# Inverted residual: the remaining 32 channels' taps on TensorE for four blocks at once, and VectorE on the second 128 channels' taps in every block but the last

## The reference

```
def _L3_conv_ref(x, w1, ..., w2, ...):          # x: (8, 48, 64, 64)
    h = relu(bn(einsum('oc,bchw->bohw', w1, x)))           # expand 48 -> 288 channels
    h = conv3x3(h, wd, padding=1, feature_group_count=288) # depthwise, one 3x3 filter a channel
    h = relu(bn(h))
    h = bn(einsum('oc,bchw->bohw', w2, h))                 # reduce 288 -> 48
    return x + h
```

## Time and profile before

| what | value |
|---|---|
| median of three runs | 1986.39 us |
| the profiled execution's own time / its span | 1985.13 / 1983.2 us |
| from the first to the last block's end in this stage | 1547.99 to 1979.00 us of the span |
| TensorE / VectorE / ScalarE busy in those 431.01 us | 399.37 / 282.46 / 170.33 us |
| mean granted TensorE clock there | 0.97 |

### The profile page before, as it was taken

One profiled execution on the slowest core, in us unless ns is written; L12 is line 12 of the kernel. 1 busy time (PEld: TensorE's weight loads), 2 busy tenths in 40 slices (PEclk: granted clock), 3 DMA queues, 4 the chain that ended last, 5 costly groups with the idle time before them and its releaser, 6 DMA issues. The chain is left out here.

```text
span 1983.2 us, 41167 instructions
## 1 busy us (share of the span) xinstructions
PE 1589.4 (80%) x13002; PEld 935.5 (47%) x13002; DVE 1475.4 (74%) x2699; ACT 1172.0 (59%) x2257; POOL 642.3 (32%) x577
## 2 busy tenths in 40 slices
PE   8979248888888888704888888888860899999997
PEld 6535125555555555203555555555520344445444
DVE  4539978888888888646888888888856766666666
ACT  1116128888888888543888888888853344444431
POOL 2010035555555555203555555555500000000000
PEclk9989669999999999857999999999985799999999
DMA  3769366666666666666666666667576011011100
GB/s 108 254 196 211 97 137 108 108 106 107 107 107 107 107 106 91 113 147 131 106 107 107 107 107 107 107 108 108 81 121 164 14 34 34 21 31 35 35 19 25
DMA packets 132266, 199.40 MB, mean 101 GB/s; under 512 B 28528, under 2 KB 47824, under 8 KB 131920
## 3 DMA queue, kind: packets, MB, share of 16 engines
q1 hardware_dynamic: 132176, 198.08, 53.7%
HBM read 73.72 MB, written 37.75 MB: 56 GB/s over the span
## 5 line engine op out<-in xcount | busy, mean ns | idle before, releaser
L720 PE MATMUL gates_l<-xh_l,w_l 128*112 128x512 f32 x3072 | 801.5, 409 | 122.3 <-ACT xh_l L757 122.1
L720 PEld LDWEIGHTS gates_l<-xh_l,w_l 128*112 128x112 f32 x3072 | 500.3, 175 | 422.8 <-issue 288.8
L684 POOL TENSOR_TENSOR xh_l<-hs,xh_l 48x512 fp32r<-48x512 f32 x252 | 300.5, 1192 | 442.0 <-ACT xh_l L757 442.0
L693 POOL TENSOR_TENSOR xh_l<-xf_l,xs_l 48x512 fp32r<-48x512 f32 x256 | 311.7, 1217 | 33.2 <-DVE xs_l L809 32.8
L720 PE MATMUL gates_l<-xc_l,w_l 128*112 128x512 f32 x512 | 164.6, 403 | 135.1 <-DVE begun_l L829 135.1
L853 DVE TENSOR_TENSOR hs<-gate_o_l,tanh_c_l 48x256 f32 (+1 forms) x512 | 193.3, 416 | 73.9 <-ACT tanh_c_l L786 70.1
L1292 PE MATMUL b_dw<-b_hid,b_diag 32*32 32x512 f32 x6840 | 235.3, 602 | 0.0
L786 ACT ACTIVATE tanh_c_l<-cell_l 48x256 f32<-48x256 f32 x512 | 158.1, 342 | 91.4 <-DVE cell_l L844 91.4
L776 ACT ACTIVATE gate_if_l<-gates_l 112x512 f32<-112x512 f32 x256 | 151.4, 591 | 99.8 <-PE gates_l L720 96.6
L844 DVE TENSOR_TENSOR cell_l<-keep_l,gates_l 48x512 f32<-48x512 f32 x256 | 178.5, 697 | 26.7
L840 DVE TENSOR_TENSOR gates_l<-gate_if_l,gates_l 48x512 f32<-48x512 f32 x256 | 178.4, 697 | 21.5
(11 more groups left out here) (150 smaller groups left out, 1436.3 us busy)
## 6 DMA issues: line engine op xcount, KB each, us to landing
xc_l<-xs_l SPq DMA_DIRECT2D x512, 99.0 KB, 3.0
xh_l<-xs_l SPq DMA_DIRECT2D x512, 66.0 KB, 2.4
xf_l<-rows SPq DMA_DIRECT2D x256, 96.0 KB, 2.2
hs<-rows SPq DMA_DIRECT2D x32, 384.0 KB, 10.3
rows<-hs SPq DMA_DIRECT2D x32, 384.0 KB, 5.1
xr<-in_x_rows SPq DMA_DIRECT2D x24, 256.0 KB, 2.7
xc<-in_x_cols SPq DMA_DIRECT2D x24, 256.0 KB, 3.0
mixed<-stage SPq DMA_DIRECT2D x24, 256.0 KB, 3.0
```

Source lines behind the costliest of these rows:

```text
L684: pool.tensor_tensor(inner(xh[n:n + C, d, 1 - s, LO, :]), whole, inner(xh[n:n + C, d, 1 - s, HI, :]).bitcast(F32), ALU.subtract).then_inc( ...
L693: pool.tensor_tensor(inner(xh[f:f + C, d, s, HI, :]), wide(xf[f:f + C, s, :]), inner(x_rows(s, slice(f, f + C))).bitcast(F32), ALU.subtrac ...
L720: return nc.tensor.matmul(ps[d][m][0:K, :], w[:, d, q, m, :], padded(tile)[:, :, lo:lo + W], start=first, stop=last)
```

## The change

The rest's taps leave VectorE. `depthwise(k, 2)` makes them on TensorE once in four blocks (k = 0, 4, 8, 12), for the sixteen rows of four blocks at once: the free dimension is 4 rows x 2 images x 64, 512 columns as in the other sets, again 144 matmuls into the four `dw` banks, and `squash(k, 2)` writes `h2_r` for four blocks. The rest must then be expanded four blocks ahead (LEAD), so the input ring has six slots and the expansions get an explicit order (EXPANDS, NUMBER): twelve before the loop. VectorE makes set 1's taps in all blocks but the last (15 blocks in place of 8; TensorE keeps one, k = 15, in place of 8). `acc_v` has two buffers, clipped in place, and `begin_v(k + 1)` moves to the end of ScalarE's block k. GpSimd makes one more part of `diag`.

```
-    XRING = 5
+    XRING = 6
+    LEAD = 4
-    PRO = 2 * EPB
+    EXPANDS = [(k, n) for k in range(2) for n in range(EPB - 1)] + [(k, EPB - 1) for k in range(LEAD)]
+    PRO = len(EXPANDS)
+    for k in range(NBLK):
+        ahead = [(k + 2, n) for n in range(EPB - 1)] if k + 2 < NBLK else []
+        ahead.insert(2 if with_rest(k) else len(ahead), (k + LEAD, EPB - 1))
+        EXPANDS += [e for e in ahead if e[0] < NBLK]
...
-            return g == 1 and k % 2 == 0
+            return g == 1 and k + 1 < NBLK
...
+                    if g == SETS:
+                        for n, (dy, dx) in enumerate(ORDER):
+                            for i in range(BLK):
+                                for j in range(BLK):
+                                    r = (j - i) % BLK
+                                    y = BLK * (k + r) + 1 + dy
+                                    mm = nc.tensor.matmul(dw[r][j * Q:(j + 1) * Q, :], diag[i * Q:(i + 1) * Q, g, 3 * dy + 3 + dx, :],
+                                                          hid_r[i * Q:(i + 1) * Q, y:y + BLK, :, dx:dx + W].rearrange("p r b w -> p (r b) w"),
...
+                    if with_rest(k):
+                        if k + LEAD < NBLK:
+                            expand(k + LEAD, EPB - 1)
+                        depthwise(k, SETS)
...
-                    if more:
-                        expand(k + 2, 4)
+                    if not with_rest(k) and k + LEAD < NBLK:
+                        expand(k + LEAD, EPB - 1)
...
+                    if k >= 2:
+                        act.wait_ge(reduced, 2 * k - 2)
...
+                    if k + 1 < NBLK and on_dve(k + 1, 1):
+                        begin_v(k + 1)
...
-                    taps(k, range(9))
-                    squash_rest(k)
```

More of the change, by code:

```diff
@@ L881, in __init__ @@
         self.wds = sb("b_wds", [P, SETS_H, 9])
-        self.diag = sb("b_diag", [P, self.SETS, 9, self.Q])
+        self.diag = sb("b_diag", [P, SETS_H, 9, self.Q])
         self.bias_h = sb("b_bias_h", [P, SETS_H])
@@ L962, in prepare @@
         bias_of(self.bias_d[:, :], self.bnd, self.td, 15)
-        for g in range(self.SETS):
+        for g in range(SETS_H):
             pool.tensor_tensor(self.diag[:, g, :, :], self.eye[:, :].unsqueeze(1).broadcast_to([P, 9, self.Q]),
@@ L974, in prepare @@
                            ALU.mult).then_inc(made, 1)
-        pool.wait_ge(made, 8)
+        pool.wait_ge(made, 9)
 def project_and_norm(nc, D, hs, rows_in, rows_out, weights, params, tag, residual=None):
@@ L1154, in inverted_residual @@
         hid_r = sb("b_hid_r", [P, H + 2, QB, WP])
[L1155 to L1158, removed]
+        acc_v = [sb(f"b_acc_v{i}", [P, BLK * B, W]) for i in range(2)]
+        h2 = sb("b_h2", [P, 2, BLK, BW])
+        h2_r = sb("b_h2_r", [P, 2 * LEAD, BLK, QB * W])
         o = sb("b_o", [P, 2, 2, BW])
@@ L1181, in on_dve @@
         def on_dve(k, g):
-            return g == 1 and k % 2 == 0
+            return g == 1 and k + 1 < NBLK
         def sets_before(k, g):
-            return sum(not on_dve(a, b) for a in range(k + 1) for b in range(SETS) if (a, b) < (k, g))
+            return sum(not on_dve(a, b) and (b < SETS or with_rest(a)) for a in range(k + 1) for b in range(SETS + 1) if (a, b) < (k, g))
         def pieces(k, dy):
@@ L1276, in depthwise @@
                 def depthwise(k, g):
-                    ahead = EPB * (k + 1) + 2 * g if k + 1 < NBLK else EPB * k + 2 * g + 1
+                    ahead = NUMBER[(k + 1, 2 * g) if k + 1 < NBLK else (k, 2 * g + 1)]
+                    if g == SETS:
+                        ahead = NUMBER[min(k + LEAD, NBLK - 1), EPB - 1]
                     pe.wait_ge(kept_a, by_act(ahead))
@@ L1283, in depthwise @@
                         pe.wait_ge(squashed_a, BLK * sets_before(k, g))
+                    if g == SETS:
+                        for n, (dy, dx) in enumerate(ORDER):
[5 more added lines that the diff above has]
+                                                          hid_r[i * Q:(i + 1) * Q, y:y + BLK, :, dx:dx + W].rearrange("p r b w -> p (r b) w"),
+                                                          start=(n == 0), stop=(n == 8), skip_group_check=True)
+                        mm.then_inc(depth, 1)
+                        return
                     for n, (dy, dx) in enumerate(ORDER):
@@ L1307, in reduce_main @@
                             r = 2 * p + h
[L1308 removed]
+                            nc.tensor.matmul(ys[p][h * HALF:(h + 1) * HALF, :], w2s[:, (0 if on_dve(k, g) else r) * SETS + g, :], clipped(k, g, r),
                                              start=(g == 0), stop=False, skip_group_check=True)
                 def reduce_rest(k, p):
+                    first = k - k % LEAD
+                    pe.wait_ge(squashed_a, BLK * (sets_before(first, SETS) + 1))
                     for q in range(QUARTERS):
@@ L1314, in reduce_rest @@
                             mm = nc.tensor.matmul(ys[p][h * HALF:(h + 1) * HALF, q * QB * W:(q + 1) * QB * W],
-                                                  w2s[:, BLK * SETS + q, :], h2_r[:, k % 2, 2 * p + h, :], start=False, stop=True,
+                                                  w2s[:, BLK * SETS + (q + k) % QUARTERS, :], h2_r[:, k % (2 * LEAD), 2 * p + h, :], start=False, stop=True,
                                                   skip_group_check=True)
                     mm.then_inc(reduced, 1)
[L1318 to L1321, removed]
+                for k, n in EXPANDS[:PRO]:
+                    expand(k, n)
+                pe.wait_ge(pads, 8)
                 for k in range(NBLK):
@@ L1372, in squash_v @@
                 def squash_v(k):
[L1373 to L1378, removed]
+                    act.wait_ge(taps_v, 8 * k + 8)
@@ L1379, in _ @@
+                    flat = acc_v[k % 2][:, :, :].rearrange("p r w -> p (r w)")
+                    nc.scalar.activation(flat, flat, ACT.Relu, bias=bias_r[:, 1:2]).then_inc(squashed_v, 1)
+                for k, n in EXPANDS[:PRO]:
+                    keep(k, n, (0,))
+                begin_v(0)
                 for k in range(NBLK):
                     more = k + 2 < NBLK
-                    if on_dve(k, 1):
-                        begin_v(k)
-                    elif k:
+                    if k:
@@ L1389, in _ @@
                     if not on_dve(k, 1):
+                        if k >= 2:
+                            act.wait_ge(reduced, 2 * k - 2)
                         squash(k, 1)
+                    if with_rest(k):
+                        if k + LEAD < NBLK:
+                            keep(k + LEAD, EPB - 1, (0, 1))
+                        squash(k, SETS)
                     if more:
@@ L1393, in _ @@
                         keep(k + 2, 3, (0, 1))
-                        keep(k + 2, 4, (0, 1))
+                    if not with_rest(k) and k + LEAD < NBLK:
+                        keep(k + LEAD, EPB - 1, (0, 1))
+                    if k + 1 < NBLK and on_dve(k + 1, 1):
+                        begin_v(k + 1)
             @block.vector
@@ L1414, in keep @@
                                             ).then_inc(kept_d, 1)
-                for n in range(PRO):
-                    keep(n // EPB, n % EPB)
+                for k, n in EXPANDS[:PRO]:
+                    keep(k, n)
                 dve.wait_ge(pads, 8)
@@ L1423, in taps_set @@
                         if n == 0:
-                            ahead = EPB * (k + 1) + 3
+                            ahead = NUMBER[k + 1, 2]
                             dve.wait_ge(kept_a, by_act(ahead))
                             dve.wait_ge(kept_d, by_dve(ahead))
-                            dve.wait_ge(begun_v, k // 2 + 1)
+                            dve.wait_ge(begun_v, k + 1)
                         else:
-                            dve.wait_ge(taps_v, 8 * (k // 2) + n)
+                            dve.wait_ge(taps_v, 8 * k + n)
@@ L1430, in taps_set @@
                         for at, slot, rows in pieces(k, dy):
                             src = hid[1][:, slot:slot + rows, :, dx:dx + W].rearrange("p r b w -> p (r b) w")
-                            part = acc_v[:, at * B:(at + rows) * B, :]
+                            part = acc_v[k % 2][:, at * B:(at + rows) * B, :]
                             nxt = nc.vector.scalar_tensor_tensor(part, src, wds[:, 1, 3 * dy + 3 + dx:3 * dy + 4 + dx], part, ALU.mult, ALU.add)
                         nxt.then_inc(taps_v, 1)
[L1436 to L1451, removed]
```

38 lines of the change are left out of this document (18 added, 20 removed).

## The result

The changed kernel took 1972.07 us (median of four, 1965.25 to 1975.82) against 1987.84: ratio 0.9922, 95% interval 0.9895 to 0.9949. A second comparison with more executions gave 0.9942, 0.9922 to 0.9963. So it is 0.6 to 0.8% faster, some 11 to 16 us, where 20 were forecast; the forecast of 1966 us is 6 under the median, inside the range. The profiled execution is the shortest of its four, 1965.25 us, so the first trace shows the change at its best.

The account below looks back on a forecast made before the run. TensorE's order and its waits for ScalarE were taken to set block length. Terms +1.7 + 1.4 + 11.9 - 9.1 - 25.1 - 0.6 = -19.8 us from 1985.13 gave 1965.3, forecast as 1966 us, range 1957 to 1977.

Parts of the forecast that it names:

- start-up, first memset to first set: Before the block loop: larger memsets for six input slots, +1.7 us, and two more rest expansions, +1.4 us.
- block 0 / block 1: First two blocks, clock partly low: block 0 gains the rest's set, +11.9 us; block 1 loses a set, -9.1 us.
- blocks 2 to 13 (one fall counted): Steady blocks: 8 x 22.0 + 2 x 33.1 + 30.0 + 20.9 = 293.1 us against 318.2, -25.1 us.
- block 14: Block without expansions: squash_v ends 0.3 us late, so 15.4 us against 15.01.
- last block's start to the last finish: Block 15: squash_v to 14.7 us, where before the reduction started at 15.6; -0.6 us together with block 14.
- The mechanism: Last stage: TensorE's order and waits for ScalarE set block length; 24 depthwise sets become 21, 29.0 us less before waits.
- the two waits of a rest block: Blocks 4 and 8: TensorE waits 1.4 and 1.0 us around the rest's expansion; block 33.1 us against 31.04.
- I leave one such in both: Blocks 2 to 13: one slow stretch, 3.63 us in place of 1.94, assumed in both kernels.
- a third dip: Clock rival, blocks 2 to 13: 3 x 1.7 us more, one or two sets at 12.08, about 1975 us; chance 0.08.
- VectorE as the bound: Rival: wide taps longer than 2.349 us, deciding from 2.57; at 2.84 the kernel takes 1993 us; chance 0.05.
- margin behind the second finish: Blocks with one set: squash_v ends 0.9 us before ScalarE's squash, 0.3 less behind a split tap, none after a rest block.
- The unknown: Price of the rest's set reading hid_r four rows at a time: 9.68 us assumed; at 12.08 in blocks 4, 8, 12, +7.2.

Follow-up runs that it names:

- same_again: The changed kernel once more with no edit, for a second trace and more executions: ratio 0.9942 to the kernel before.
- half_sets: Changed kernel, but VectorE makes set 1 in even blocks only, as before; the rest's taps stay on TensorE: 2024.65 us, ratio 1.0202 to before.
- vector_both: Changed kernel with the rest's taps back on VectorE, which also keeps set 1; TensorE makes 17 sets: 1989.65 us, ratio 1.0034 to before.
- fill: Changed kernel plus two discarded TensorE matmuls inside the 1.37 us wait of blocks with one set: ratio 0.9891 to before.
- more_after: Changed kernel plus one 1.81 us VectorE operation in each block, behind the second finish, ahead of the last three taps: ratio 1.0068 to before.
- rest_early: Changed kernel with the rest's expansion first behind the depthwise step and its set ahead of the second expansion, in rest blocks: ratio 0.9931 to before.

## Why the prediction was right in kind and where it was off

| step | predicted | first trace | same_again |
|---|---|---|---|
| start-up, first memset to first set | 28.2 | 26.1 | 26.1 |
| block 0 / block 1 | 36.4 / 24.3 | 36.2 / 24.1 | 36.2 / 24.2 |
| blocks 2 to 13 (one fall counted) | 294.8 | 297.2 | 305.0 |
| block 14 | 15.4 | 15.4 | 15.4 |
| last block's start to the last finish | 37.2 | 37.9 | 37.6 |
| stage | 436.3 | 436.9 | 444.4 |

That the first trace meets the sum within 0.6 us is partly luck: its start-up came out 2.1 us shorter than computed and its blocks 2 to 13 longer by 2.4.

- *The mechanism* was right: TensorE's order with its waits sets the blocks, three sets less arrive minus the two waits of a rest block. half_sets and vector_both show that neither half alone gains anything.
- *The mis-sized term* is the clock, "I leave one such in both". Before has one fall in either trace; after has one in its blocks with one set in one trace and four in the other, 1.6 to 1.8 us each, and three of the four sets of blocks 4 and 8 took 11.1 to 12.4 us. That is the whole difference of 7.5 us between the two traces' stages. That it is also the gain that the median lacks is likely, not shown: the mean granted clock of the whole execution is 0.931 in the profiled one and 0.925 to 0.927 in the three longer ones, but none of these has a trace. The rival "a third dip", at 0.08, is what happens in most traces of this kernel and its near relatives; fill shows it by taking the waits away. I had also miscounted: before has six even blocks with this wait (2 to 12), not seven, so its trace showed one fall in six. The Trainium skill, "TensorE: Matmul & The Clock Gate", section "A second HAM failure mode: psum-queue depth-cycling", tells of a kernel whose clock swings because TensorE idles briefly and often between groups of matmuls. The runs agree more than I allowed, four of nine blocks in same_again, but no run of the changed kernel has it in every block.
- *Start-up* cost 1 us, not 3, and neither term was the right one. From the first memset to the third expansion it is 15.3 us against 13.2, 2.1 more where 1.7 was counted; the memsets are as computed (3.47 us each against 2.62). From there to the first set it is 10.8 us against 12.0, 1.1 less where 1.4 more was counted. The two further expansions took the 0.67 us each that the sum had for them, but the clock was full from the fifth expansion on, while before made three further wide ones at the low clock. Before, then after:

```profile
1540.78 2.08 PE L1265 MATMUL b_ys<-b_xs,b_w1s 48*128 48x512 f32 x4
1542.64 1.92 PE L1265 MATMUL b_ex<-b_xs,b_w1s 48*128 48x512 f32 x4
...
1541.30 1.12 PE L1278 MATMUL b_ex<-b_xs,b_w1s 48*128 48x512 f32 x4
1542.47 1.13 PE L1278 MATMUL b_ys<-b_xs,b_w1s 48*128 48x512 f32 x4
```

- *VectorE as the bound* didn't happen. Its margin behind the second finish is as small as I said: more_after overruns it by 0.7 us and, with the falls that follow, is slower than before.
- *The unknown.* The rest's set costs 9.68 us like the others where the clock is full (blocks 8 and 12); reading four rows of `hid_r` costs nothing more.

## What to carry to other kernels

Slack is a place, not a sum: lay out one period between the points at which two engines meet, and ask what stands behind the last of them. When a change takes work from TensorE in every second block, price the granted clock as well, since more blocks then hold a short wait; and fill those waits, with work that has to be done anyway or even with discarded matmuls. Merging two into one doesn't help: behind the one of 2.61 us in rest_early the clock fell too. When a wait is moved, write down TensorE's whole order behind it: two expansions next to each other gave the won time back.

## What the runs showed that was not expected

The clock fell after waits as short as 1.37 us, in an execution here and not there, with the same instructions (22.0 or 23.8 us for one block). Two discarded matmuls of 64 x 512 in that wait made the kernel 0.5% faster. The stages of the changed kernel's two traces differ by 7.5 us from the clock alone. As much and more lies ahead of the stage, which the change hardly touches: it began at 1522 in the first trace and at 1517 in same_again, and between 1517 and 1528 over all fourteen traces. This was not looked into. So where a gain is a few us, the stage's length in the trace says more than the time of the execution, and two traces say more than one.
